# Output projection and token routing on Trainium2: group sizes, the engine of the variances, and an early load of x

## The reference

```python
x = x + attention(layernorm(x))        # 16 heads of 16, rope, causal softmax, projection with bias
x = x + experts(layernorm(x))          # 8 experts, each 256 -> 1024 -> 256

# experts, for tokens t = layernorm(x):
aff = t @ centroids.T
assign = argmax(aff, axis=1)           # one expert for each token
alpha = sigmoid(aff[assign])
h = layernorm(t, ln_g[e], ln_b[e])
y = t + relu(h @ w1[e].T + b1[e]) @ w2[e].T + b2[e]
out = alpha * y + (1 - alpha) * t
```

## Time and profile before

| what | value |
|---|---|
| median of 3 runs | 892.99 us (892.44 to 894.5) |
| the profiled execution, its own time | 890.49 us |
| its span, first to last instruction | 888.7 us |
| granted TensorE clock, mean over the span | 0.985 |
| TensorE busy | 835.6 us, 94% |
| VectorE busy | 597.9 us, 67% |
| ScalarE busy | 497.6 us, 56% |
| POOL busy | 327.6 us, 37% |

### The profile page before, as it was taken

The page is one execution under the profiler, slowest core; times in us unless marked ns, Lnnn a source line. Parts: engine busy times, 40 slices in busy tenths (PEclk is TensorE's granted clock), DMA queues, the critical chain, the costliest instruction groups (busy, mean ns, idle before and its releaser), DMA issues. The chain is left out here.

```text
span 888.7 us, 24625 instructions
## 1 busy us (share of the span) xinstructions
PE 835.6 (94%) x8767; PEld 524.4 (59%) x8768; DVE 597.9 (67%) x1133; ACT 497.6 (56%) x1168; POOL 327.6 (37%) x469
## 2 busy tenths in 40 slices
PE   6999859999989999999999988789999999999995
PEld 4555433444434444434444434569999999999994
DVE  4888999898878898988888902966433333333331
ACT  4668426777767777777877795024333333333330
POOL 9999663343233434324243431634111111111111
PEclk9999988999999999999999999999999999999998
DMA  8578632553433333322333323968555555555540
GB/s 280 156 234 260 180 110 77 175 169 87 107 87 87 98 87 99 81 79 72 89 92 96 113 41 101 294 236 256 199 182 178 177 177 178 182 183 178 177 173 0
DMA packets 62643, 129.50 MB, mean 146 GB/s; under 512 B 16217, under 2 KB 43482, under 8 KB 56282
## 3 DMA queue, kind: packets, MB, share of 16 engines
q1 hardware_dynamic: 58282, 112.99, 42.4%
q0 software_dynamic: 4272, 15.29, 4.7%
HBM read 100.35 MB, written 23.44 MB: 139 GB/s over the span
## 5 line engine op out<-in xcount | busy, mean ns | idle before, releaser
L891 ACT ACTIVATE arena<-ps_pair 128x512 f32<-128x512 f32 (+2 forms) x640 | 308.6, 565 | 99.9 <-PE ps_pair L1214 96.7
L971 DVE TENSOR_REDUCE B_block_max<-ps_item 128x8 f32<-128x1024 f32 x288 | 338.1, 1220 | 32.4 <-PE ps_item L1118 31.4
L1214 PE MATMUL ps_pair<-q_stack,k_stack 99*32 99x512 bf16 (+7 forms) x3072 | 191.5, 333 | 9.2 <-ACT arena L891 5.5
L805 POOL TENSOR_SCALAR_AFFINE_SELECT arena<-arena 128x256 f32<-128x256 f32 x256 | 102.9, 408 | 164.5 <-ACT arena L891 160.3
L1214 PEld LDWEIGHTS ps_pair<-q_stack,k_stack 99*32 99x32 bf16 (+1 forms) x3072 | 79.0, 96 | 134.0 <-ACT arena L891 88.6
L1231 PE MATMUL ps_pair<-arena,B_v_quad 128*32 128x512 f32 (+3 forms) x1536 | 153.9, 494 | 1.2 <-ACT B_oacc L910 0.5
L1855 PEld LDWEIGHTS C_bank<-arena 128*128 128x128 f32 x1248 | 146.1, 193 | 1.9
L1855 PE MATMUL C_bank<-arena 128*128 128x128 f32 x1248 | 146.4, 276 | 0.0
L1875 PE MATMUL C_ps_p<-arena 128*128 x624 | 141.0, 379 | 0.0
L1875 PEld LDWEIGHTS C_ps_p<-arena 128*128 128x128 f32 x624 | 115.6, 190 | 14.1
L1507 ACT ACTIVATE arena<-C_bank,ffn_columns 128x128 f32<-128x128 f32 x156 | 44.5, 368 | 141.7 <-PE C_bank L1855 141.7
(11 more groups left out here) (168 smaller groups left out, 672.6 us busy)
## 6 DMA issues: line engine op xcount, KB each, us to landing
arena<-in_w_exp SPq DMA_DIRECT2D x41, 1024.0 KB, 5.0
qk_parts<-arena SPq DMA_DIRECT2D x32, 384.0 KB, 3.4
q_stack<-qk_parts SPq DMA_DIRECT2D x96, 128.0 KB, 3.0
k_stack<-qk_parts SPq DMA_DIRECT2D x64, 128.0 KB, 3.0
arena<-in_w_exp POOLq DMA_DIRECT2D x6, 1024.0 KB, 6.9
rows<-payload SPq DMA_DIRECT2D x39, 130.5 KB, 2.1
arena<-in_x SPq DMA_DIRECT2D x8, 512.0 KB, 5.1
arena<-in_x_feat SPq DMA_DIRECT2D x8, 512.0 KB, 6.1
```

The source lines that it names most:

```text
L805: pool.affine_select(out=block_p, in_=block_p, compare_op=ALU.is_ge, fill=0.0, base=0, pattern=[[0, 2], [1, P]], channel_multiplier=-1).th ...
L891: act.activation(pr[s % PR][:, h:h + 2 * n - 1:2, 0:W], ps_s[(EXPS * Q.const + exps_to[s] + u) % R][:, 0:n * W].rearrange("p (h n) -> p h ...
L971: dve.tensor_reduce(bmx[:, g:QH:GH, first:first + 3 * gap + 1:gap], src[:, :, :].rearrange("p c (b n) -> p c b n", n=P), AX.X, ALU.max).th ...
L1214: mm = pe.matmul(bank[at:at + 32, :], ks[rows, r, half, bass.ds(g * SEQ + kb * P + at, 32)], qs[rows, r, half, bass.ds(g * SEQ + c * QW + ...
```

## The change

The groups of tiles become 8, 8, 6, 6 and 4, of which the first two precede the first table. `positions` and `row_scalars` of a group (but the last two) come three pairs behind its last pair, and the one-hots right behind its last pair for the first two groups. The mean and variance of pairs 1, 3, 5, 7, 9, 11 and 13 are taken by ScalarE, with two passes over each tile (a copy with its sum, a square with its sum); VectorE keeps the other nine. The first eight tiles of x are loaded to a free place of the arena in the last step of attention, and the loads of the other tiles go behind `place_out`. On ScalarE the reads of four expert numbers and the statistics of pair 13 now stand behind the first `normalize`. Left out of the diff are the hunks that only pass the new names on.

```diff
@@ -40,8 +40,8 @@
 REGION = NTOK + P
 DUMMY_ROW = NE * REGION
 G = KB
-GROUPS = (4, 4, 4, 4, 6, 6, 4)
-FIRST_GROUPS = 4
+GROUPS = (8, 8, 6, 6, 4)
+FIRST_GROUPS = 2
 FIRST_SLOTS = 8
 RD = 4
 COL_S, COL_B, COL_K, COL_GATE, COL_ID = range(DIM, DIM + 5)
@@ -143,6 +143,8 @@
                   for at in [OUT_AT_WEIGHTS * W2C] + [late + b * KB * DIM for b in range(BATCH - 1)]]
         o_late = arena[:, INV_AT_WEIGHTS * W2C:(INV_AT_WEIGHTS + 1) * W2C].rearrange("p (a n) -> p a n", a=2)
         inv_all = o_late[:, 1, :]
+        x_early = arena[:, late + (BATCH - 1) * KB * DIM:late + BATCH * KB * DIM].rearrange("p (t n) -> p t n", t=KB)
+        s_xe0 = sem("first_x_rows_loaded")
         den = ctx.enter_context(nc.sbuf_tensor("out_sums", [P, 2, 2, SEQ * QH // P], F32))
         inv_d = dram("inverse_sums", [NQ, QH, SEQ], F32)
         s_late = sem("last_second_weights_loaded")
@@ -231,6 +233,11 @@
             b, c = divmod(pair, DC)
             eng.tensor_tensor(o_feat[b][:, c, :], o_feat[b][:, c, :], inv_all, ALU.mult).then_inc(s_nm, 1)
 
+        def load_early(sp):
+
+            sp.wait_ge(s_vq, NQ)
+            sp.dma_start(x_early[:, :, :], x[0:KB * P, :].rearrange("(t p) n -> p t n", p=P)).then_inc(s_xe0, 16)
+
         def load_w1(sp, S):
             e = sp.value_load(slot_tab[0:1, 0, bass.ds(S.value(), 1)], min_val=0, max_val=NE - 1)
             sp.dma_start(w1b[:, S.ring(2), :],
@@ -714,6 +721,8 @@
                             sp.dma_start(pay_d[e * REGION:e * REGION + P, :], padrow).then_inc(s_pad, 16)
                     if n.const >= 3:
                         spread_inverse(sp, n.const - 3)
+                    if n.const == NQ - 1:
+                        load_early(sp)
                     Q = n + 2
                     if Q.within(NQ):
                         load(Q)
@@ -1268,13 +1277,21 @@
         starts = [sum(GROUPS[:g]) for g in range(NG + 1)]
         FIRST = GROUPS[:FIRST_GROUPS]
         FT = sum(FIRST)
-        assert starts[NG] == NT and all(k % 2 == 0 and k <= G for k in GROUPS) and all(k == 4 for k in FIRST)
+        assert starts[NG] == NT and all(k % 2 == 0 and k <= G for k in GROUPS)
+        ends_at = [starts[g + 1] // 2 - 1 for g in range(NG)]
+        BY_ACT = [u for u in range(NP - 1) if u % 2 == 1]
+
+        def tiles_by(act, u):
+
+            return 2 * sum((m in BY_ACT) == act for m in range(u))
+
         assert (FT * P - NE * (P - 1) + P - 1) // P >= FIRST_SLOTS
         REST = NSLOT - FIRST_SLOTS
 
         xr = sb("x_rows", [P, NT, PAYW])
         st = sb("st", [P, R, 6])
         mv = sb("mv", [P, NT, 2])
+        am = sb("shares_of_mean", [P, NT])
         sd = sb("sd", [P, 3, NT])
         eps2 = sb("eps2", [P, 1])
         top = sb("top", [P, NT])
@@ -1303,6 +1320,7 @@
         HC = FC // 2
         zz = room[:, 0:2 * DIM].rearrange("p (r n) -> p r n", r=2)
         xT = room[:, 2 * DIM:4 * DIM].rearrange("p (r c n) -> p r c n", r=2, c=DC)
+        junk = room[:, 4 * DIM + FF:4 * DIM + FF + 2 * DIM].bitcast(BF16).rearrange("p (a n) -> p a n", a=4)
         hr = room[:, 4 * DIM:4 * DIM + 2 * FF].rearrange("p (r c n) -> p r c n", r=2, c=FC)
         y = sb("y", [P, 2, DIM])
         al = sb("al", [P, 2, 3])
@@ -1323,6 +1341,9 @@
         s_lg = sem("logits_pair")
         s_bn = sem("bn_stats")
         s_v = sem("variance")
+        s_am = sem("mean_by_act")
+        s_va = sem("variance_by_act")
+        s_ma = sem("means_scaled")
         s_sd = sem("sqrt")
         s_rs = sem("reciprocal")
         s_sb = sem("row_scalars")
@@ -1376,12 +1397,11 @@
         with nc.Block() as block:
             @block.sync
             def _(sp):
-                for h in range(2 * NT // G):
+                place_out(sp, NQ - 1, o_last)
+                for h in range(2, 2 * NT // G):
                     t = h * G // 2
                     sp.dma_start(xr[:, t:t + G // 2, 0:DIM],
                                  x[t * P:(t + G // 2) * P, :].rearrange("(t p) n -> p t n", p=P)).then_inc(s_x[h], 16)
-                    if h == 0:
-                        place_out(sp, NQ - 1, o_last)
                     if h == 4:
                         store_inverse(sp, NQ - 1)
                     if h == 5:
@@ -1458,7 +1478,8 @@
                 known = {}
 
                 def roots(g):
-                    act.wait_ge(s_v, starts[g + 1])
+                    act.wait_ge(s_v, tiles_by(False, starts[g + 1] // 2))
+                    act.wait_ge(s_va, tiles_by(True, starts[g + 1] // 2))
                     act.activation(sd[:, 0, of(g)], mv[:, of(g), 1], ACT.Sqrt, bias=eps).then_inc(s_sd, 1)
                     if g == 0:
                         act.wait_ge(s_pre, 6)
@@ -1473,17 +1494,33 @@
                         act.activation(zz[:, S.ring(2), :], row[:, 0:DIM], ACT.Identity, bias=row[:, COL_B:COL_B + 1],
                                        scale=row[:, COL_S:COL_S + 1]).then_inc(s_zz, 1)
 
-                for w in range(NP):
-                    if w == NP - 1 - RD:
+                def stats(u):
+                    act.wait_ge(s_x2, u + 1)
+                    for t in (2 * u, 2 * u + 1):
+                        i = t % 2
+                        act.activation(junk[:, i, :], xr[:, t, 0:DIM], ACT.Copy, scale=1.0 / (HD * DIM),
+                                       accum_out=am[:, t:t + 1]).then_inc(s_am, 1)
+                    if tiles_by(True, u):
+                        act.wait_ge(s_va, tiles_by(True, u))
+                    for t in (2 * u, 2 * u + 1):
+                        done = tiles_by(True, u) + t % 2 + 1
+                        act.wait_ge(s_am, done)
+                        act.activation(junk[:, 2 + t % 2, :], xr[:, t, 0:DIM], ACT.Square, bias=am[:, t:t + 1], scale=-1.0 / HD,
+                                       accum_out=mv[:, t, 1:2]).then_inc(s_va, 1)
+                    act.activation(mv[:, 2 * u:2 * u + 2, 0], am[:, 2 * u:2 * u + 2], ACT.Copy, scale=float(HD)).then_inc(s_ma, 1)
+
+                for u in range(NP - 1):
+                    if u == NP - 3:
+                        act.wait_ge(s_fl, 32)
                         act.wait_ge(s_tab, 2)
-                    if NP - 1 - RD <= w < NP - 1:
-                        expert_of(act, Step(w - (NP - 1 - RD)), known)
+                        normalize(Step(0))
+                        for S in range(RD):
+                            expert_of(act, Step(S), known)
+                    if u in BY_ACT:
+                        stats(u)
                     for g in range(NG - 2):
-                        if w == starts[g + 1] // 2 + (1 if g < FIRST_GROUPS else 3):
+                        if u == ends_at[g] + (0 if ends_at[g] in BY_ACT else 1):
                             roots(g)
-                act.wait_ge(s_fl, 32)
-                act.wait_ge(s_tab, 2)
-                normalize(Step(0))
 
                 def turned_rows(S):
                     if S.within(NSLOT):
@@ -1543,21 +1580,23 @@
                 def add(u):
                     n, at = 2 * u + 1, 2 * u % R
                     two = xr[:, n - 1:n + 1, 0:DIM]
+                    before = x_early[:, n - 1:n + 1, :] if n < KB else two
                     dve.wait_ge(s_pj, n + 1)
-                    dve.wait_ge(s_x[2 * n // G], 16)
-                    dve.tensor_tensor(two, ps_p[:, at:at + 2, 0:DIM], two, ALU.add).then_inc(s_x2, 1)
+                    dve.wait_ge(s_xe0 if n < KB else s_x[2 * n // G], 16)
+                    dve.tensor_tensor(two, ps_p[:, at:at + 2, 0:DIM], before, ALU.add).then_inc(s_x2, 1)
                     dve.tensor_tensor(xl[:, n - 1:n + 1, :], ps_p[:, at:at + 2, DIM:DIM + NE], xl[:, n - 1:n + 1, :],
                                       ALU.add).then_inc(s_lg, 1)
 
                 def stats(u):
+                    before = tiles_by(False, u)
                     dve.wait_ge(s_x2, u + 1)
-                    if u >= 2:
-                        dve.wait_ge(s_v, 2 * u - 2)
-                    for t in (2 * u, 2 * u + 1):
-                        dve.bn_stats(st[:, t % R, :], xr[:, t, 0:DIM]).then_inc(s_bn, 1)
-                    for t in (2 * u, 2 * u + 1):
-                        dve.wait_ge(s_bn, t + 1)
-                        dve.bn_aggr(mv[:, t, :], st[:, t % R, :]).then_inc(s_v, 1)
+                    if before >= R:
+                        dve.wait_ge(s_v, before + 2 - R)
+                    for i in range(2):
+                        dve.bn_stats(st[:, (before + i) % R, :], xr[:, 2 * u + i, 0:DIM]).then_inc(s_bn, 1)
+                    for i in range(2):
+                        dve.wait_ge(s_bn, before + i + 1)
+                        dve.bn_aggr(mv[:, 2 * u + i, :], st[:, (before + i) % R, :]).then_inc(s_v, 1)
 
                 def one_hot(g):
                     r, k = g % 2, GROUPS[g]
@@ -1595,6 +1634,7 @@
 
                 def row_scalars(g):
                     dve.wait_ge(s_sd, 2 * (g + 1))
+                    dve.wait_ge(s_ma, tiles_by(True, starts[g + 1] // 2) // 2)
```

(39 more changed lines are left out.)

2 lines of the change are left out of this document (1 added, 1 removed).

## The result

| | before | changed |
|---|---|---|
| median | 891.82 us (13 runs, 887.81 to 894.5) | 895.63 us (13 runs, 890.23 to 898.21) |
| ratio | 1 | **1.0043**, 95% interval 1.0023 to 1.0063 |
| span of the profiled execution | 888.7 us | 893.5 us |
| first projecting matmul of the stage | 545.07 | 545.77 |
| from there: first scatter / sixteenth scatter starts | 13.48 / 34.51 | 19.60 / 38.77 |

The changed kernel is slower by 3.8 us (2.1 to 5.6). 3.3 us of it stand in the profile between the first projecting matmul and the end of the first slot's products; the rest of the span's 4.8 us is a start 0.7 us later and 0.8 us in the slots.

A forecast was written before the change was run, and what follows sets the result against it. The prediction took VectorE and POOL as near their limit together, and POOL's scatters as the bound after the change. Scatters +1.2 us and a longer cold stretch +0.9 gave +2.1 on 893.0: 895.1 us, range 892.0 to 898.5 for 8 in 10.

The forecast's parts named there:

- the forecast's own: Whole kernel: the forecast case, slower by +1.8 to +3.5 us, 894.8 to 896.5 us; chance 0.48.
- The scatter queue: POOL's first sixteen scatters: first 6 us later, at 564.6; 1.26 us apart; sixteenth at 584.0 against 579.58.
- The change of group: POOL between the first two groups of eight scatters: 0.75 us idle instead of 0.30.
- Landing: Sixteenth scatter's landing: 2.7 us instead of 5.91, bounds 2.6 and 5.91; first rows normalized at 589.75, +1.2 us.
- The clock: TensorE from the first rows' transposes through pair 15: half clock after one long wait, 0.9 us from the longer cold stretch.
- ScalarE's order: ScalarE's reads and pair 13's statistics behind its first normalizing: ready at 596.0, TensorE wants it at 597.9, hidden.
- A second cover: VectorE's normalizing of the last outputs: inverse sums there by 566.8 at latest; costed at nothing, at most 0.2 us.
- the prediction's signs of being wrong: Traces: scatters closer than 1.26, first before 562, VectorE waiting at line 232, ScalarE later than pair 15, slot before 599.4.
- In the slots: Later groups of 6 and 4 tiles behind the slots: as now, costing nothing.
- B: POOL's scatters: spacing closes from 1.26 to 0.96 us as VectorE's load lightens, kernel faster, 891.0 us; chance 0.08.
- A: Whole kernel: same scatters, clock returns early or falls late, no visible change, +0.2 to +1.8, say 893.9; chance 0.31.
- C: Sixteenth scatter: landing still takes 5.91 us behind weight loads, clearly slower, +5.3 us, 898.3; chance 0.13.

The follow-up runs named there:

- E1: Changed kernel with the old groups (4, 4, 4, 4, 6, 6, 4), early x and ScalarE's variances kept; ratio 1.0011 to the kernel before.
- E3: Changed kernel with x loaded as before, no early load; ratio 1.0052 to the kernel before.
- E7: E6 with TensorE's pair 15 and its number reads ahead of the transposes of the first rows; ratio 0.9997 to the kernel before.
- E9: Changed kernel with 14 unread TensorE products (6 and 8) put in its two waits; ratio 1.0049 to the kernel before.
- E2: Kernel before with only the early load of eight x tiles and the later x loads behind the placing; ratio 0.9971.
- E8: E7 with groups (4, 4, 4, 4, 6, 6, 4); ratio 0.9973 to the kernel before.
- E10: E1 with the first four groups' rank products one pair and positions two pairs behind a group's last pair; ratio 1.003 to the kernel before.
- E12: Kernel before with E2's early x and E7's order on TensorE, groups and variances as before; ratio 0.9928, 884.75 us against 892.25.
- E6: Changed kernel with ScalarE's four number reads and pair 13's statistics ahead of its first normalizing; ratio 1.0026 to the kernel before.
- E5: Changed kernel with 26 unread TensorE products (10 and 16) put in its two waits; ratio 1.0043 to the kernel before.
- E11: E10 with E7's order between the first rows and the first slot; ratio 1.0002 to the kernel before.
- E4: Changed kernel with all variances on VectorE; ratio 1.0044 to the kernel before.

## Why the prediction was right, point by point

**Direction and chain.** Forecast +2.1 us (0.2%), measured +3.8 (2.1 to 5.6): the right direction, inside the wide range, and just above the forecast's own +1.8 to +3.5. That the median of 895.63 us lies so close to the 895.1 foretold is partly luck: the kernel before came out at 891.82 over 13 runs, not at the 892.99 that the forecast was added to.

**The scatter queue.** Foretold from the first matmul (545.07): first scatter 19.5, sixteenth 38.9. Measured 19.60 and 38.77. The trace shows it, and E1, where the sizes alone were undone, brings the two 4.8 and 2.7 us forward; how much of that reaches the total lies between its trace (0.5) and its medians (2.9). The change of group, put at 0.75 us of idle time, was 0.31, as between most scatters.

**Landing.** Taken as 2.7 us, it was 3.44, and load and hand-over 3.28 instead of 3.05. So the rows were normalized 0.8 us later than foretold (45.49 against 44.68). That the landing would be shorter was right, and the traces of all fourteen kernels show what it goes with. In the seven kernels with groups of eight (changed, E3 to E7, E9) the sixteenth scatter starts 5.8 to 6.2 us after the issue of slot 0's first weights and lands in 2.8 to 3.5 us. In the seven with groups of four (before, E1, E2, E8, E10 to E12) it starts only 1.0 to 1.3 us after that issue and lands in 5.5 to 7.4 us. (For E6, E7 and E12 this is the time to the issue of the rows less 0.83 us.) With groups of eight the table is ready at the tenth scatter, where before it was ready at the fourteenth, so the weights' load is further ahead of the last scatter. That wins back more than half of what the late first scatter costs: 4.3 us at the sixteenth are 1.8 at the issue of the rows. That the weights' load is the reason is argued; no run moves it alone.

**The clock.** Right in kind: half clock from the transposes on. It came back 5.8 us after the resumption of pair 15 at 594.36, where I had transferred 4.8. I had not foretold the first fall at 580, which was covered because TensorE was waiting for rows afterwards anyway. The price is the 2.7 us of E5; that it is worth as much in the total is argued, not shown. The rule of the Trainium skill (TensorE: Matmul & The Clock Gate, "HAM oscillation"), that a burst behind a wait for a DMA starts throttled, agrees with this trace: 0.50 in all of pair 15. E1's trace agrees in part: behind 2.33 us of wait for the rows its transposes still took 0.41 us, as at full clock, and only pair 15 was slow (3.89).

**ScalarE's order.** Foretold ready 1.9 us before TensorE wants it. In the trace the second pass of reads shows as 1.82 us of issue, and the scaled rows are there at 596.85, TensorE wants them at 599.0: covered by 2.2. It is a cover that only the slow pair 15 gives, and E6 did not settle it.

**A step that held in the profiled execution and not in others: "A second cover ... costed at nothing, at most 0.2".** A wait of VectorE at the normalizing (line 232, now 234) was among the prediction's signs of being wrong, and it came. In the changed kernel, VectorE in order of time, where before stood:

```profile
567.01 1.23 DVE L234 TENSOR_TENSOR arena<-arena 128x1024 f32<-128x1024 f32 x1 [1.09 <-DMA arena<-inverse_sums]
```

That wait was 1.09 us and hidden, but the two numbers meet closely: the second group's scatters were due at 575.69 and its scalars were done 0.9 us before. The profiled executions of E5, E6, E7 and E9, which have the same code up to there, show what a microsecond more does. E5, VectorE and POOL's ninth scatter:

```profile
566.34 1.23 DVE L234 TENSOR_TENSOR arena<-arena 128x1024 f32<-128x1024 f32 x1 [2.57 <-DMA arena<-inverse_sums]
```

```profile
577.79 0.99 POOL L1457 DMA_INDIRECT payload<-C_x_rows,C_posi  x1 [4.34 <-issue]
```

and E9:

```profile
568.52 1.22 DVE L234 TENSOR_TENSOR arena<-arena 128x1024 f32<-128x1024 f32 x1 [2.03 <-DMA arena<-inverse_sums]
```

| from the first matmul | changed | E6 | E9 | E7 | E5 |
|---|---|---|---|---|---|
| normalizing starts | 21.24 | 21.97 | 22.18 | 22.19 | 22.73 |
| TensorE's wait for the one-hots behind it, us | 0.38 | 1.10 | 1.31 | 1.33 | 1.86 |
| pair 10's products, us | 2.05 | 2.05 | 3.02 | 3.63 | 3.73 |
| POOL idle before the ninth scatter, us | 0.31 | 0.30 | 1.14 | 1.75 | 4.34 |
| sixteenth scatter | 38.77 | 39.50 | 40.59 | 41.22 | 43.06 |

In E9, E7 and E5 TensorE's clock falls behind this wait (0.50 in 574 to 576 us of E9), and pair 10 takes 3.02 to 3.73 us instead of 2.05. The length of the wait alone does not decide it: the kernel before stood 1.55 us until 572.24, and its next pair took 2.05. The fall is what multiplies the delay; that is how 0.9 and 1.5 us at the normalizing became 1.8 and 4.3 at the sixteenth scatter. The forecast had bounded the arrival at 21.7, a little short, and priced it without the clock. The sum over the profiled execution was short by 1.2 us, all from landing and clock; that the median is 0.5 us above even that fits these waits, but no kernel took the wait away from the changed one, so it stays an argument.

**A step that was left out: the scatter beside the normalizing.** In E6 POOL has no gap, and yet its sixteenth scatter is 0.73 us later. The third one took 1.76 us instead of 1.03:

```profile
568.85 1.23 DVE L234 TENSOR_TENSOR arena<-arena 128x1024 f32<-128x1024 f32 x1 [1.82 <-DMA arena<-inverse_sums]
```

```profile
569.14 1.76 POOL L1457 DMA_INDIRECT payload<-C_x_rows,C_posi  x1 [0.30 <-issue]
```

It started while VectorE was normalizing the last outputs, and ended 0.82 us behind it. So it is in twelve of the fourteen traces: the one scatter that starts during this instruction ends 0.82 to 0.84 us behind the instruction's end, whatever its start, and takes up to 1.97 us (E9) and 1.99 (E7); in E10 and E11 none starts there. The kernel before has it too, beside the normalizing at 569.98 of the earlier trace rows, in a scatter that the earlier trace rows leave out:

```profile
570.54 1.48 POOL L1437 DMA_INDIRECT payload<-C_x_rows,C_posi  x1 [0.30 <-issue]
```

In the changed kernel it cost 0.07 us, because the scatter and the normalizing barely met.

**In the slots** 0.8 us came that I had put at nothing, 0.50 of it TensorE's wait in slot 2: the weights are asked for 0.75 us after slot 0's products, as before, and take 7.4 us with the next load and the scatters of the last groups beside them. E2's execution has the same 0.50, so it does not need the new groups.

**The rivals.** B fell: the 0.30 us between two scatters stayed in every kernel here, with VectorE half idle. But its reason was put aside too quickly. The prediction took from two rows that VectorE does not hold POOL's scatters up, and the one instruction above does. The lock-out that the Trainium skill describes (DMA: Bandwidth & Descriptors, "SWDGE vs HWDGE vs iDMA") fits it: the scatter seems to stand until VectorE's instruction is over. The page ties it to a mode of VectorE's instructions, and whether this one is in it no run here shows. The price is once per kernel and at most 1.03 us here. A, no change that shows, is E1's case. C's last landing of 5.9 us did not come in the changed kernel, nor in any other with groups of eight.

## What to carry to other kernels

A bigger batch saves its fixed work on one engine and delays the first item to the next: where the next engine has a fixed rate (here 1.26 us for a scatter, sixteen in a row) and never runs dry, the start of its first item sets the end, and a saving upstream that does not bring this start forward is worth nothing. Before moving work off an engine, look for work that can go into a wait that exists: pair 15 in the wait for the first rows gave 3.8 us in E12 (against E2) and 4.1 in E7 (against the changed kernel), more than any other single gain here. When a rule is tested on rows, look for the row where it would bite: two quiet rows did not rule out the one long scatter. A wait put down as hidden should be priced with what stands behind it in its queue and with the clock of the engine that then stands still.

## What the runs showed of the hardware that was not expected

The attention part, the same code in all of these kernels but for one load, ended between 541.66 us (E2) and 546.88 us (E6) in single profiled executions. Differences of single spans under 5 us say nothing. Times from the stage's own first matmul repeat to 0.01 us up to the first scatter (19.60 in the changed kernel and in E4, E5, E6, E7 and E9); behind the inverse sums they no longer do (sixteenth scatter 38.77 to 43.06 in the same kernels). And one chip was 12 us slower: in the traces of E5 to E8 298.1 to 301.1 us lie behind the end of the first slot's products, in all the others 289.3 to 290.1. Nothing in the core's own record explains it.
